# An attention phase in gated steps: q's halves made a tile earlier, and the state's decay as one product with a column that GpSimd spreads

## What is computed

```python
ge = jnp.exp(g_t)
hk = hk * ge[:, :, None, :] + k_t[..., :, None] * s_t[..., None, :]
logits = jnp.einsum('bhk,bhkm->bhm', q_t * scale, hk)
p = jax.nn.softmax(logits, axis=-1)
hv = hv * ge[..., :, None] + s_t[..., :, None] * v_t[..., None, :]
o_t = jnp.einsum('bhm,bhmv->bhv', p, hv)
```

## Time and profile before

| | |
|---|---|
| median of three runs | 3056.42 us (3054.19 to 3059.04) |
| the profiled execution, its own time | 3053.13 us |
| its span, first to last instruction | 3051.4 us |
| mean granted TensorE clock | 0.993 |
| PE busy | 2910.8 us (95%), weight loads 2557.7 us (84%) |
| DVE, ACT, POOL busy | 2669.0 (87%), 1854.0 (61%), 2043.7 us (67%) |

### The profile page before, as it was taken

The page is one execution under the profiler, slowest core; times in us unless marked ns, Lnnn a source line. Parts: engine busy times, 40 slices in busy tenths (PEclk is TensorE's granted clock), DMA queues, the critical chain, the costliest instruction groups (busy, mean ns, idle before and its releaser), DMA issues. The chain is left out here.

```text
span 3051.4 us, 102767 instructions
## 1 busy us (share of the span) xinstructions
PE 2910.8 (95%) x34624; PEld 2557.7 (84%) x34624; DVE 2669.0 (87%) x4370; ACT 1854.0 (61%) x5448; POOL 2043.7 (67%) x3191
## 2 busy tenths in 40 slices
PE   5999999999999999788999999998899999999999
PEld 4888888888888888678888888888788888888888
DVE  7999999999999998477888888887899999999998
ACT  2777777777777777767777777776222222222222
POOL 5788888888888887356666666666555555555553
PEclk9999999999999999899999999999999999999999
DMA  4455555555555555456666666665333333333332
GB/s 107 114 138 138 137 137 138 137 138 137 137 138 137 137 138 134 155 142 167 179 175 175 177 179 175 175 179 149 89 77 76 76 76 76 76 76 76 76 76 58
DMA packets 814248, 387.11 MB, mean 127 GB/s; under 512 B 586068, under 2 KB 748244, under 8 KB 814168
## 3 DMA queue, kind: packets, MB, share of 16 engines
q1 hardware_dynamic: 814168, 386.07, 49.0%
HBM read 184.49 MB, written 134.22 MB: 104 GB/s over the span
## 5 line engine op out<-in xcount | busy, mean ns | idle before, releaser
L777 PE MATMUL banks<-ffn_xT_hl,w_hl 128*128 128x128 f16 x12288 | 729.7, 219 | 0.0
L499 PE MATMUL banks<-w_hl,midT_hl 128*128 128x256 f16 x6144 | 712.5, 273 | 6.6 <-DVE low_hl L696 6.0
L777 PEld LDWEIGHTS banks<-ffn_xT_hl,w_hl 128*128 128x128 f16 x12288 | 704.2, 98 | 3.9 <-issue 0.6
L499 PEld LDWEIGHTS banks<-w_hl,midT_hl 128*128 128x128 f16 x6144 | 595.4, 98 | 75.7 <-DVE midT_hl L690 7.8
L669 DVE TENSOR_TENSOR_SCAN runmax<-restart,banks 128x1024 f32<-128x1024 f32 x256 | 585.6, 2287 | 8.1 <-PE banks L756 0.2
L608 ACT ACTIVATE midT_hl<-banks 128x1024 f16<-128x1024 f32 x256 | 262.1, 1024 | 300.8 <-PE banks L789 300.8
L690 DVE SCALAR_TENSOR_TENSOR midT_hl<-banks,midT_hl 128x1024 f16<-128x1024 f32 x256 | 312.0, 1219 | 90.9 <-ACT midT_hl L608 90.9
L298 POOL TENSOR_TENSOR ffn_xT_hl<-ffn_xT,ffn_xT_hl 128x256 f16<-128x256 f32 x256 | 190.0, 742 | 279.6 <-ACT ffn_xT_hl L293 277.0
L674 DVE TENSOR_TENSOR step<-runmax 128x1024 bf16<-128x1024 f32 x256 | 338.8, 1323 | 8.9
L499 PE MATMUL banks<-wqkfv_hl,att_xT_hl 128*128 128x512 f16 (+1 forms) x1536 | 293.7, 328 | 2.0 <-issue 1.4
L614 ACT ACTIVATE low_hl<-banks 128x128 f16<-128x128 f32 x256 | 70.3, 275 | 352.8 <-PE banks L499 352.8
(11 more groups left out here) (141 smaller groups left out, 6826.5 us busy)
## 6 DMA issues: line engine op xcount, KB each, us to landing
projected<-qkvf_out SPq DMA_DIRECT2D x128, 384.0 KB, 2.4
ffn_xT<-ffn_blocks SPq DMA_DIRECT2D x1024, 32.0 KB, 2.0
gates_d<-gates_out SPq DMA_DIRECT2D x128, 256.0 KB, 2.8
gates<-gates_d SPq DMA_DIRECT2D x128, 256.0 KB, 3.7
qkv<-projected SPq DMA_DIRECT2D x128, 256.0 KB, 2.8
x_in<-in_L_attn_x SPq DMA_DIRECT2D x128, 128.0 KB, 2.6
x_res<-in_L_attn_x SPq DMA_DIRECT2D x128, 128.0 KB, 2.3
x<-x_out SPq DMA_DIRECT2D x128, 128.0 KB, 2.2
```

The lines of the kernel that those rows point to most:

```text
L499: last = nc.tensor.matmul(dst, left(lp, k), right(rp, k), start=(k == 0 and lp == rp), stop=(k == blocks - 1 and lp == 1))
L777: nc.tensor.matmul(mid_ps[t.slot][:, cols], w1_hl[:, wp, k, cols], xT_hl[:, t.ring, xp, k], start=(c % PER_BANK == 0 and k == 0 and wp == xp),
```

## The change

1. `q_high` on ACT and `q_low` on POOL work on tile s+2 instead of s+1. On ACT q_high moves from the head of the step to between softmax_exp and o_high; on POOL q_low moves from the head of the step to behind weight.
2. POOL gets a new stage, `spread_column` for tile s+1, between q_low and own_decay: own_column = own_head times decay_col, both broadcast, 128 x 256 values.
3. DVE's `decay_Hv` becomes one tensor_tensor product of 256 columns, state_sum times own_column, and waits for own_column in place of decay_col.

```diff
+                def spread_column(t):
+
+                    if t.chunk:
+                        after_chunk(pool, S["decay_col_made"], t, LATER)
+                        after_chunk(pool, S["Hv_made"], t, LATER, lag=2)
+                        nc.gpsimd.tensor_tensor(
+                            own_column[:, t.slot],
+                            own_head[:, :].rearrange("p (a c) -> p a c", a=1).broadcast_to([P, PAIRS, P]),
+                            decay_col[:, t.ring].rearrange("p (a c) -> p a c", c=1).broadcast_to([P, PAIRS, P]),
+                            ALU.mult).then_inc(S["own_column_made"], 1)
...
-                return Phase([(q_low, 1), (rms, -2), (weight, 0), (own_decay, 2), (o_low, -4)],
+                return Phase([(rms, -2), (weight, 0), (q_low, 2), (spread_column, 1), (own_decay, 2), (o_low, -4)],
...
-                        after_chunk(act, S["Hv_made"], t, LATER, lag=4)
+                        after_chunk(act, S["own_column_made"], t, LATER, lag=4)
...
-                return Phase([(q_high, 1), (evacuate_PtT, -1), (evacuate_T, 1), (square_sums, -2),
-                               (softmax_exp, 0), (o_high, -4), (exp_sums, 2)],
+                return Phase([(evacuate_PtT, -1), (evacuate_T, 1), (square_sums, -2),
+                               (softmax_exp, 0), (q_high, 2), (o_high, -4), (exp_sums, 2)],
...
-                        after_chunk(dve, S["decay_col_made"], t, LATER)
+                        after_chunk(dve, S["own_column_made"], t, LATER)
...
-                        for a in range(PAIRS):
-                            last = nc.vector.scalar_tensor_tensor(
-                                state[:, t.slot, 1, a], state_sum[:, 1, a], decay_col[:, t.ring, a:a + 1],
-                                own_head[:, :], ALU.mult, ALU.mult)
-                        last.then_inc(S["Hv_made"], 1)
+                        nc.vector.tensor_tensor(state[:, t.slot, 1], state_sum[:, 1], own_column[:, t.slot],
+                                                ALU.mult).then_inc(S["Hv_made"], 1)
```

More of the change, by code:

```diff
@@ L878, in attention_phase @@
             decay_own = fb("decay_own", [P, 4, D])
+            own_column = fb("own_column", [P, 2, PAIRS, P])
             decay_col = fb("decay_col", [P, 4, PAIRS])
@@ L1383, in build @@
             "inv_total_made", "Pt_made", "PtT_done", "PtT_made",
-            "update_done", "state_sum_made", "Hk_made", "Hv_made",
+            "update_done", "state_sum_made", "Hk_made", "Hv_made", "own_column_made",
             "o_done", "o_raw_made", "o_sum_made", "o_sum_eps_made", "o_rms_made",
```

## The result

| | before | changed |
|---|---|---|
| median of 9 runs each, us (range) | 3055.59 (3053.61 to 3059.04) | 3066.38 (3062.22 to 3067.99) |
| profiled execution, us (span) | 3053.13 (3051.4) | 3065.39 (3063.5) |
| period of four tiles at 1720 us | 26.05 | 26.59 |
| its steps 0, 1, 2, 3 | 6.98, 6.85, 6.09, 6.13 | 6.84, 6.92, 6.53, 6.30 |

The ratio is 1.0034, 95% interval 1.0023 to 1.0044: slower by 10.8 us, where 15.6 were forecast.

What follows compares the result with a forecast made beforehand. PE, busiest, waits ahead of products_A mostly for DVE's k_low behind Hv, slowed by POOL collisions. Steps sum to 26.42, with carry 26.60: +0.55 a period x 28.7 = +16 us, about 3072; 8-in-10 range 3025 to 3092.

Steps and rivals of the forecast that it cites:

- step 0: First step of the four-tile period: column ahead of St, decay_own and Hk delayed, 6.93 us (was 6.98).
- step 1: Second step of the period: column ahead of St, decay_own and Hk delayed, 6.79 us (was 6.85).
- step 2: Third step, without decay_own: column ahead of St, Hk behind o_low, 6.73 us (was 6.09).
- step 3: Last step of the period: products_A follows k_low, no longer q_low, 5.97 us (was 6.13).
- carry: Shorter Hv leaves o_raw's chain to Pt nearer the next products_A: 0.06 to 0.20 us in steps 0 to 2, 0.06 taken.
- the ties: POOL's column against DVE's St, starts within 0.03 us in steps 1 and 2: POOL first in 0, likely 1, 2 open.
- one step won and the other lost: Case of DVE winning only one of steps 1 and 2: 3050 to 3060 us, no change to be told.
- DVE comes first: Rival: St starts before the column in steps 1 and 2, period 25.78, 3048.6 us; ties shared or won by DVE 0.22.
- PE's waits ahead of A: Sign: PE's wait before products_A stays near 2 us a period and is for DVE's k_low.
- The start and the end of the phase stay: Claim that the attention phase's start and end, like both feed-forward phases, keep their time.
- No collisions to speak of: Rival: POOL's products mostly miss DVE's, period 24.65, -40 us, 3016; chance 0.25 for 3010 to 3046.
- The carry feeds itself: Rival: late turn_o delays o's moves, o_high and expnG, so St slips with the column: 3084 to 3092; over 3090 0.03.

Runs made afterwards that it cites:

- e3: The changed kernel with spread_column moved to the end of POOL's step, a tile further ahead: 3035.21 us, ratio 0.9942 to the kernel before.
- e4: The changed kernel with the column's product replaced by a memset and a four-column product, Hv not decayed: 3027.36 us, ratio 0.9919 to the kernel before.
- e5: The kernel before plus two unused POOL products of 256 columns between weight and own_decay: 3103.26 us against 3055.27, ratio 1.0157.
- e9: The changed kernel with o_high on ACT moved behind exp_sums: 3047.76 us, ratio 0.9972 to the kernel before.
- e2: The changed kernel with q's halves back at the head of the step, one tile ahead: 3051.63 us, ratio 0.9993 to the kernel before.
- e1: The kernel before with only q's halves moved two tiles ahead, Hv still two instructions: 3037.86 us against 3053.49, ratio 0.9954.
- e8: The kernel before with q's halves two tiles ahead, o_low held until Hv is made, and o_high behind exp_sums: 3004.43 us, ratio 0.9826.

## Why the prediction came out right, and where its steps were off

The mechanism held: an instruction of DVE that reads two arrays and a product of POOL that reads don't overlap, the collision moved from Hv to St and Hk, and e3, e4 and e5 show it from three sides. The period was 26.59 where 26.60 had been forecast, and that closeness is mostly luck. By its parts:

| | forecast | measured | what was different |
|---|---|---|---|
| step 0 | 6.93 | 6.84 | St first, not the column; Hv met oT |
| step 1 | 6.79 | 6.92 | as forecast, but PE follows Hk by 1.60 |
| step 2 | 6.73 | 6.53 | St first, but later than in the kernel before by 0.22 |
| step 3 | 5.97 | 6.30 | St met q_low |
| carry | 0.18 | in the rows above | |

With the ties as they fell (the column first in step 1 alone) the forecast's own sums give 6.93 + 6.79 + 6.21 + 5.97 and the carry of 0.18, a period of 26.08 at most, since its 6.93 is for the column first in step 0: no change. It had said so, 3050 to 3060 for "one step won and the other lost". What made up for it were 0.32 in step 2 and 0.33 in step 3 that the sum did not have.

*The ties.* Forecast: POOL first in steps 0 and 1, step 2 open and counted for POOL. Measured: POOL by 0.01 in step 1, DVE by 0.05 in step 0 and by 0.11 in step 2. In step 0 Pt started 2.47 after A, not 2.36, so q_low and the column slid by 0.11, and St, which hangs on expnG, did not. The forecast laid this carry to the shorter Hv, but step 3, which goes before, has no Hv: there A no longer waits for q_low, so the end of o_raw lies 1.40 ahead of A and not 1.52. It put the carry on top of each step's sum, as time; the first effect was to turn who comes first. Once St is first, Hk is still caught, as the rival "DVE comes first" had it for steps 1 and 2: the column has been waiting and gets in between St and Hk. It ends at 4.62 and Hk at 4.91, where 5.42 had been worked out for step 0. The half microsecond that this saved was mostly given back by Hv, which met oT (0.84) and was thought to be free there.

*Step 2.* The rival's chain for it (St to 3.95, column 4.43, Hk 4.70, A at 6.21) is the one that ran, all of it later: 4.18, 4.65, 4.93 and 6.53. POOL is later because Pt starts 2.53 after A and not 2.22; it waits for prob. A now starts right behind the matmuls of the logits, so logit on DVE starts 0.10 after A, where it started 0.18 ahead of it, and the softmax is late by that. Behind Pt q_low runs until 3.90, so St cannot end much before 4.18 whatever expnG does: e9's step 2 shows it.

*The wait that was not in the sum.* From Hk's end to A the forecast took 1.51, by way of Hv and k_low. PE has its own way from Hk, the products of the state in the logits, which is 1.60 long in steps 1 and 2 (1739.32 to 1740.92). PE in step 1 of the changed kernel:

```profile
1739.46 0.46 PE L1277 MATMUL banks<-state,qkv 128*128 128x128 f32 x2 [0.30 <-DVE state L1186]
...
1740.92 0.29 PE L1257 MATMUL banks<-qT_hl,kT_hl 64*128 64x128 f16 x4
```

A no longer waits at all there; the lateness stands one group of matmuls earlier. With 5.32 + 1.60 step 1 closes at its 6.92, and step 2 with Hk's end at 4.93 + 1.60 at its 6.53. The forecast said that PE's waits ahead of A would stay near 2 us a period, behind k_low. They are 0.69 (0.42 and 0.27), and 0.72 stands elsewhere (0.30 and 0.19 for Hk, 0.23 for St): wrong in place. Two more of its signs failed: St is at 0.43 in steps 0 and 2, not at 0.7 to 1.0, and step 3 got longer by 0.17, not shorter by 0.16.

*Step 3.* This was the term of the sum that failed most, by 0.33. The forecast gave the moved q_low a price in steps 0 to 2, together with the column, and none in step 3, where it counted only the wait that goes away. Its own rule would have given one, by the rows of the kernel before: Pt starts 2.50 after A, so q_low would run from about 3.17 to 3.84; St, from 3.41, would meet it and end at 4.12, and 4.12 + 2.13 makes 6.25. Measured are 4.16 and 6.29 or 6.30. e9 takes the 0.32 away by bringing St ahead of q_low.

The forecast read the gap that covers q_high on ACT in step 1 alone, and in step 3 that gap is not there. ACT in step 3 of the kernel before (A at 1740.19):

```profile
1742.88 0.42 ACT L1097 ACTIVATE oT<-oT 128x256 f16<-128x256 f32 x1 [0.27 <-DMA oT<-o_blocks]
1743.20 0.37 ACT L1041 ACTIVATE expnG<-banks 128x256 f32<-128x256 f32 x1
```

But that did no harm: in step 3 o_high starts 2.88 after A with q_high in front and 2.89 without it, in e2, since the moves of o come late in both. They come late because turn_o stands behind the delayed Hk (it ends 1.18 ahead of A, not 1.40). expnG is 0.20 late by that, and it costs next to nothing, as q_low holds St anyway: e4, with expnG at 3.03, has a step 3 of 6.25.

*The size.* From the nineteenth A to the one numbered 125 the changed kernel took 2119.76 - 1415.23 = 704.53 us, the kernel before 2104.47 - 1415.00 = 689.47: +15.06, the forecast's +16. What had been left out is the end of the phase. The last three steps took 24.37 us before and 21.12 now. A's of before, then of the changed kernel:

```profile
2110.57 0.51 PE L1248 MATMUL banks<-qT_hl,kT_hl 64*128 64x128 f16 x12 [0.66 <-POOL qT_hl L1031]
...
2118.90 0.55 PE L1248 MATMUL banks<-qT_hl,kT_hl 64*128 64x128 f16 x12 [1.81 <-POOL qT_hl L1031]
...
2128.84 0.51 PE L1248 MATMUL banks<-qT_hl,kT_hl 64*128 64x128 f16 x12 [2.27 <-POOL qT_hl L1031]
```

```profile
2125.92 0.51 PE L1257 MATMUL banks<-qT_hl,kT_hl 64*128 64x128 f16 x12 [0.42 <-issue]
...
2140.88 0.51 PE L1257 MATMUL banks<-qT_hl,kT_hl 64*128 64x128 f16 x12 [0.69 <-issue]
```

There A really did wait for q_low, for 2.27 us at the last, and q made two tiles ahead is worth 3.25. The runs agree: these three steps take 20.22 us in e1, which has q ahead, and 24.42 in e2, which has not. "The start and the end of the phase stay" was the wrong sentence. 15.06 + 0.23 - 3.25 = 12.04 us is the difference of the last A's starts, and the two profiled executions differ by 12.26.

*The rivals.* "No collisions to speak of" is what e3 and e4 come near to (25.53 and 25.30): the price of 3016 that the forecast gave it was out of reach, since 24.65 also needed an Hv that meets nobody and a step 3 of 5.97. e8 is at 24.68: its step 3 takes 5.92, and there no POOL product stands in front of Hv, which is still two instructions. "The carry feeds itself" happened in its first links, from the late turn_o to the moves, o_high and expnG, but in steps 2 and 3 q_low held St in any case, so it did not feed on: the period stays at 26.59.

*Still open.* In steps 0 of all these kernels St starts 0.33 to 0.34 after the end of the copy of 512 columns ahead of it, and expnG was ready some 0.2 before; no run here tells why. In step 2 of the kernel before it follows the sum of 512 columns by 0.12, with expnG ready. What remains ahead of A at the end of each step 3, 0.41 us, was not tried either.

## What to carry to other kernels

An idle stretch on one engine is free only if what the other engine does beside it doesn't read through the same way: before filling it, list the neighbour's instructions that read two arrays from SBUF, and count how many products fit before the first of them. Where a pair of instructions is slow, see first whether it is the work or what it meets: here a wait of 0.8 us on the idle engine was worth more than halving the work, and an edit that gained 15.6 us alone and one that cost nothing alone lost 10.8 together, because both used one gap. Work out what a moved instruction meets in each step of the period, also in the step where it takes a wait away, and look at the run-in and run-out of the phase on their own. Where a run can be explained by both the theory and its rival, as e9 can, look for another run in which only one of them is changed: e4 was that run here.

## What the runs showed of the hardware

Besides the written order and the semaphores a third thing sets here when work is done: what DVE and POOL read at the same time.

- The prices of a meeting are steady in all the rows shown: a blocked DVE instruction of 128x256 ends 0.27 to 0.29 us after the POOL product that blocks it; a blocked POOL product ends 0.46 to 0.60 after the DVE instruction.
- Who starts first wins, in the rows shown down to 0.01 us (1737.55 against 1737.56).
- An instruction that waits gets in as soon as the other ends, even between two that follow back to back: decay_own was behind the column on POOL at once, and St ran between them.
- POOL's product with one operand constant along the row took 0.61 us (608 ns at the least), one with both operands full 0.72 to 0.73, as the forecast had assumed. A memset of the same size took 0.30 and did not lengthen Hk beside it (0.41).
